# A preln graph layer on one core: three groups of ScalarE instructions change places in the edge step

## The reference

```python
h  = max(layernorm(x), 0)
em = relu(LN(concat(h[src], h[dst]) @ msg_w + msg_b) * msg_g + msg_beta) * edge_weight
messages = segment_mean(em, dst)                   # zero where no edge arrives
gate  = sigmoid(h @ gate_w + gate_b)
h_new = relu(LN(concat(h, messages) @ upd_w + upd_b) * upd_g + upd_beta)
out   = x + gate * h_new + (1 - gate) * h
```

## Time and profile before

| | us |
|---|---|
| three runs | 982.22, 986.97, 993.64 |
| their median | 986.97 |
| the profiled execution, own time | 981.87 |
| its span, first to last instruction | 980.1 |

### The profile page before, as it was taken

The page is one execution under the profiler, slowest core; times in us unless marked ns, Lnnn a source line. Parts: engine busy times, 40 slices in busy tenths (PEclk is TensorE's granted clock), DMA queues, the critical chain, the costliest instruction groups (busy, mean ns, idle before and its releaser), DMA issues.

```text
span 980.1 us, 19229 instructions
## 1 busy us (share of the span) xinstructions
PE 698.9 (71%) x3696; PEld 547.5 (56%) x3696; DVE 873.4 (89%) x3834; ACT 852.0 (87%) x3678; POOL 673.0 (69%) x602
## 2 busy tenths in 40 slices
PE   2377787877777777886766377777867878687781
PEld 1255555555555555554555266666756766576661
DVE  7299999999989999999995379999998888879984
ACT  3299999999989999999996389999989888779963
POOL 4667777776876877878747566766766666666557
PEclk9655655565555555556567698999899889889976
DMA  5246666666666667667523112333221111111111
GB/s 150 90 147 216 203 215 218 204 222 204 227 223 213 215 219 239 222 220 237 174 67 103 51 43 88 97 98 97 77 75 65 64 59 62 65 64 60 57 70 34
DMA packets 74260, 133.65 MB, mean 136 GB/s; under 512 B 15846, under 2 KB 17718, under 8 KB 74194
## 3 DMA queue, kind: packets, MB, share of 16 engines
q1 hardware_dynamic: 53868, 97.58, 28.6%
q0 software_dynamic: 18912, 34.84, 13.0%
q10 hardware_dynamic: 1414, 0.53, 0.2%
HBM read 56.01 MB, written 80.81 MB: 140 GB/s over the span
## 4 chain that ended last, share of the span: by engine, by line
ACT 45%; DVE 23%; issue 12%; PE 9%; another core or an unknown queue 6%; POOL 3%; ACTq 1%; DVEq 0%; DMA 0%; POOLq 0%; SPq 0%
ACT junk L410 13%; ACT hrow L403 9%; ACT work L437 8%; DVE work L458 5%; DVE work L469 5%; ACT xload L403 4%; POOL out L615 3%; DVE work L480 3%; ACT lnv L385 3%; DVE st L357 3%; ACT work L1134 2%; DVE work L475 2%; ACT rs L390 2%; PE pm L1273 2%
## 5 line engine op out<-in xcount | busy, mean ns | idle before, releaser
L615 POOL DMA_INDIRECT out<-work,sidx x196 | 201.4, 1027 | 128.0 <-issue 55.0
L1221 PE MATMUL pt<-ident,hrow 128*128 128x128 f32 x508 | 128.3, 401 | 128.9 <-ACT hrow L403 108.8
L610 POOL DMA_INDIRECT ring<-in_x,gidx x140 | 171.0, 1221 | 60.7 <-issue 41.1
L437 ACT ACTIVATE work<-work,gt 128x128 f32<-128x128 f32 x588 | 200.7, 413 | 3.7 <-DVE work L475 3.3
L1255 PE MATMUL py<-w_u,work 128*128 128x129 f32 x784 | 200.0, 434 | 0.0
L1255 PEld LDWEIGHTS py<-w_u,work 128*128 128x128 f32 x784 | 171.6, 322 | 39.2 <-issue 39.2
L610 POOL DMA_INDIRECT ring<-in_x,src_i x116 | 143.0, 1233 | 46.4 <-issue 34.4
L1221 PEld LDWEIGHTS pt<-ident,hrow 128*128 128x128 f32 x508 | 84.8, 202 | 159.3 <-ACT hrow L403 135.6
L410 ACT ACTIVATE junk<-py 128x128 bf16<-128x128 f32 x588 | 152.5, 278 | 18.5 <-remote 14.0
L469 DVE SCALAR_TENSOR_TENSOR work<-py,rs,g_upd 128x128 f32<-128x128 f32 x588 | 162.9, 336 | 4.2 <-ACT rs L390 4.2
L403 ACT ACTIVATE hrow<-xload,nb,rs 128x128 f32<-128x128 f32 x392 | 161.9, 489 | 3.0 <-DVE nb L396 2.7
(11 more groups left out here) (172 smaller groups left out, 1631.9 us busy)
## 6 DMA issues: line engine op xcount, KB each, us to landing
xload<-in_x SPq DMA_DIRECT2D x98, 256.0 KB
normalised_rows<-hrow SPq DMA_DIRECT2D x98, 256.0 KB
out<-work SPq DMA_DIRECT2D x98, 256.0 KB
running_sums<-acc SPq DMA_DIRECT2D x49, 256.0 KB
staged_target_rows<-work SPq DMA_DIRECT2D x14, 256.0 KB
ring<-staged_target_rows SPq DMA_DIRECT2D x14, 256.0 KB
out<-work,sidx POOLq DMA_INDIRECT x196
ring<-in_x,gidx POOLq DMA_INDIRECT x140
```

Source lines behind the costliest of these rows:

```text
L437: last = nc.scalar.activation(t_buf[:, g.at % 4, k, :], t_buf[:, g.at % 4, k, :], ACT.Relu, scale=gt[:, g.at % 4, k:k + 1])
L610: pool.indirect_dma_start(out=dest, out_offset=None, in_=rows, in_offset=bass.IndirectOffsetOnAxis(ap=idx, axis=0), **({} if rows is sums_ ...
L615: pool.indirect_dma_start(out=out, out_offset=bass.IndirectOffsetOnAxis(ap=idx, axis=0), in_=rows, in_offset=None, **if_tail).then_inc(s, 16)
L1221: last = nc.tensor.transpose(dest[:, k * H:(k + 1) * H], rows[:, k, :], ident[:, :])
```

## The change

It changes places in ScalarE's `edge_step` alone. `post` of s-6 moves from behind the third evacuation to ahead of the first one; the evacuation of `pa` moves from ahead of `post` to behind the first rows of L403. In the steps that have no node part the new order is: L385, L390, post (L410 on `py`, L418), L1132, L1134, L403 (first part), L1074, L427, L403 (second part), and the rest as before.

```diff
@@ edge_step of ScalarE
                     logs(act, nd, node, 2 * G)
                     rstds(act, nd, node, 2 * G)
+                if live(s.back(6), EG):
+                    post(act, ed, s.back(6), (s.at + 1) % 4, 3 * G, G, 1.0)
                 g = s.back(2)
                 if live(g, EG):
                     ed["flip"].after(act, g, 1)
...
                     if live(node.back(6), NG):
                         gated_relu(act, nd, node.back(6))
-                g = s.back(5)
-                if live(g, EG):
-                    evacuate(ed, g, at_[:, g.at % 2, :], pa[:, :], ACT.Copy, "at", "aflip")
-                if live(s.back(6), EG):
-                    post(act, ed, s.back(6), (s.at + 1) % 4, 3 * G, G, 1.0)
                 g = s.back(1)
...
                 if node is not None:
                     node_h(node)
+                q = s.back(5)
+                if live(q, EG):
+                    evacuate(ed, q, at_[:, q.at % 2, :], pa[:, :], ACT.Copy, "at", "aflip")
                 if live(s.back(6), EG):
                     gates(act, s.back(6), 0)
```

## The result

Slower. Four runs of the changed kernel have a median of 1004.65 us (997.89 to 1006.34), four of the kernel before in the same comparison 990.31 us (982.22 to 997.27); the ratio is 1.0158, with a 95% interval of 1.0080 to 1.0236. That is some 15 us, where the forecast was 7, and just inside the upper end of the range (1005.0). Every ratio in this document leaves out runs that are over 1.5% above the fastest of their kernel, so it can differ from that of the medians. The profiled execution of the changed kernel took 997.89 us, with a span of 996.2 and a granted clock of 0.688 over it (before: 980.1 and 0.706).

What follows compares the result with a forecast made beforehand. ScalarE and GpSimd's mean round were taken as level in the first stretch, GpSimd's round as the bound in the second; 5.1 + 2.0 + 0.3 = 7.4 us on 986.97 gave 994.4, rounded to 994.0, range 977 to 1005.

Steps and rivals of the forecast that it cites:

- the second stretch: Late edge-phase rounds set by GpSimd: four slow-clock rounds cost 3 x 1.2 + 1.54 = 5.1 us.
- the filled-wait rival: At L1134's idle time: upd is not held with flip 2, post runs inside the wait; 10 us faster, 977; chance 0.20.
- The move of the sums: Sums evacuated behind L403's first rows: cost 0 in the rounds, at most 1.6 us a step.
- the drain: Steps 51 to 53, where the sums' evacuation is directly on the path: 0.3 us slower, bounds 0 and 2.
- At full clock … 7.74, still inside 8.16: cost 0: Release to flip 2 grows from 6.20 by 1.54 to 7.74 us, within GpSimd's one-gather round of 8.16: no cost.
- with two gathers (9.47) nothing: At half clock the lengthened path of 9.3 us costs nothing against GpSimd's two-gather round of 9.47.
- The low-clock round with one gather: At half clock the path of 9.3 us passes GpSimd's 8.16: some 1.2 us a round.
- The first stretch: Edge-phase steps where ScalarE and GpSimd's mean round are level: ScalarE wants its first mark 0.48 earlier; 2.0 us slower.
- the bound of 3.8: Upper limit of the first stretch's cost: eight steps that stall today, 8 x 0.48 = 3.8 us.
- TensorE's marks reach the others only when GpSimd's run of indirect transfers is over: Edge phase: marks are released about 2.1 us behind the start of GpSimd's last gather, closing a round of 8.16 or 9.47.
- The rival of the held message mark: Before the squares on `pm`: the message product's mark is held too; 9 us more, 1003; chance 0.15.
- Lateness in one round is partly paid back by the next: Across rounds: the reason given for rounding the forecast from 994.4 to 994.0 us.

Runs made afterwards that it cites:

- e1: Only post moved ahead of the evacuations, the sums' evacuation left behind L1134, against the kernel before: 1030.47 us against 1014.5, ratio 1.0150.
- e11: post placed between the evacuations L1132 and L1134, sums evacuated right behind L1134, against the kernel before: 998.11 us against 993.2, ratio 1.0048.
- e2: Only the sums' evacuation moved behind the first rows of L403, post left in place, against the kernel before: 1013.67 us, ratio 0.9995.
- e5: The whole new order from step 50 on alone, otherwise the kernel before: 990.75 us against 993.2, ratio 0.9992.
- e7: Kernel before with GpSimd's 52 refill gathers replaced by plain loads on SyncE (wrong rows, same work for other engines): 964.2 us against 989.47, ratio 0.9746.
- e6: The whole new order in steps 30 to 49 alone, otherwise the kernel before: 997.41 us against 989.47, ratio 1.0105.
- e14: The whole new order in steps 8 to 29 alone, otherwise the kernel before: 999.82 us against 992.47, ratio 1.0069.
- e8: Changed kernel with the refill gathers replaced by plain loads on SyncE (wrong rows): 976.81 us, ratio 0.9868 to the kernel before.
- e13: Kernel before without GpSimd's wait for flip 2 of group g+6, so runs of two groups can join: 1065.96 us against 993.2, ratio 1.0720.
- e9: Changed kernel with TensorE turning the sums four times in place of once: 1002.24 us against the kernel before's 989.47, ratio 1.0148.

## Why the prediction was right or wrong

**What held.** The sign, the place and, in the second stretch, the mechanism. There most of TensorE's marks leave some 2 us behind the start of GpSimd's last gather, upd together with flip 2 (903.93 in the timeline above), so `post` did not fit into the wait and came onto the path: the filled-wait rival fell (e1, e11). The path itself was sized right: from release to flip 2 I had 7.74 at full clock and 9.3 at the lower one, and the profile of after has 903.28 - 895.50 = 7.78, and 832.67 - 823.31 = 9.36 in the round with a clock of 0.81. The move of the sums costs nothing that can be seen (e2), nor does the drain (e5), for which I had 0.3. The forecast of what the profile would show mostly came true: idle time before the first squares on `py`, one-gather rounds at the lower clock near 9 us, `hrow`'s waits gone; but full-clock ones are not all "still 8.1". The Trainium skill ("Perfetto Trace Analysis", Tensor Engine Instruction) says that a matmul's end in a profile is an estimate, so the matmuls themselves might be late. This trace speaks against it: in a round that isn't held ScalarE starts 0.04 behind the estimated end, three marks whose matmuls end 0.43 apart arrive 0.06 apart, and without the gathers ScalarE waits for flip 2 in 4 of steps 31 to 44 and not in all 14, in three of them 0.04 behind the matmul (e7).

**What failed: the size of two terms.** Both were 7.1 us together and measure 17 (10.4 and 6.8).

*The second stretch, "At full clock … 7.74, still inside 8.16: cost 0" and "with two gathers (9.47) nothing".* I had 5.1 from four rounds at the lower clock; e6 measures 10.4. The path was compared with GpSimd's round as if the two ran apart and the longer one counted. They share a mark, and who is released by it changes from round to round. A start that TensorE sets has GpSimd begin 1.18 behind ScalarE in place of 0.81, so the round is 8.43 to 8.50 and not 8.04 to 8.15 even at full clock, and the one with two gathers 9.87 and not 9.46 to 9.52. Each such start costs up to 0.4; there are five, 1.8 us in all. The low-clock round with one gather was priced at 1.2; the three of them cost 8.95 - 8.1 = 0.85 each. With two gathers it was priced at nothing: three times that is so (9.50 to 9.54, at a clock of 0.82), and once, at 0.67, it took 10.35, 0.85 over the 9.5 of before. The prediction had the slow rounds mostly with one gather; in this profile four of the eight have two. The eighth, behind the last gather, was not in the sum and is the dearest: 8.94 in place of 7.13, 1.8 us. Together that is some 7 us; less the 1.1 that before itself loses in its round at 0.63 (9.17 from 854.78 on) it is the 6 by which the fourteen rounds differ. The windows of six rounds above show each kind. Steps 45 to 49, which I left out, lose 2.5 (36.8 to 39.3), in two places: step 45 takes 8.86 in place of 7.44, which is mostly this last round, and step 49 takes 8.16 in place of 7.09. Steps 46 to 48 take 7.44 in both: the loop of 7.34 leaves 0.1 a step in which a lateness could be regained.

*The first stretch, "Here ScalarE comes to L1134 mostly later than the mark … I take 2.0".* e14 measures 6.8, over the bound of 3.8, which its interval only just reaches. The bound counted the eight steps that stalled before and multiplied them by 0.48, the earlier want of a mark. But 1.54 is also added to the loop of ScalarE and TensorE, and at the lower clock that loop (7.34 at full clock, 8.92 in the round at 0.81) passes ScalarE's own step, which is 8.64 by the stages and was 8.75 in the prediction. The path of 9.3 at the lower clock stood in the prediction too, and was set against GpSimd alone. e8 shows this without gathers: steps of 8.9 to 9.0, and of 10.3 to 10.6 behind a longer low stretch, where e7 has 8.64.

*"TensorE's marks reach the others only when GpSimd's run of indirect transfers is over"* is too general. The first rows of the timeline above have a mark in the midst of a run: the last product for `py` ends at 603.38, and ScalarE starts at 603.46, 0.61 behind the start of a gather that takes 1.02. In e13 too the mark of 849.25 is passed on at 849.29, between the scatters of 848.88 and 850.17. By the semaphores' records of after, 24 of 32 marks of the message product whose matmul ends between two transfers of a run are there within 0.1 us. In the second stretch upd and flip 2, which end under the run's last transfers, are mostly held; what decides it no run here shows.

*The rival of the held message mark* was seen once in the profile of after: at step 26 ScalarE waits 2.94 us for `pm`, whose product had ended at 744.66, until 748.11, 2.34 behind the start of the gather of 745.77; and five times, 3.1 us in all, for the product itself. The profile of e14 has it once too, 1.53 us. It looks like a small part, but no run takes it out, and that it explains some us of the 15 can't be excluded.

*"Lateness in one round is partly paid back by the next"* held less than thought: to regain a lateness a full-clock round had 8.16 - 6.20 = 1.96 us before, and has 8.16 - 7.78 = 0.38 after.

**What stays open.** How the rise of the time at the lower clock (68 to 85 us) and the loss feed each other; the doses (5 us for 1.06, 15 for 1.54) look like it, and e9 speaks against the clock as the whole reason, but e9 is not clean. And the split between the switches and the low-clock rounds is read from one profile of each kernel, not measured by a run. Why some marks are held under a run and others pass is open as well.

## What to carry to other kernels

When an engine's wait looks like room for other work, ask what ends the wait: if the mark for the work comes in the same moment as the mark that is waited for, the work goes onto the path and not into the gap. Then set the longer path against every loop that shares a mark with it, at the lower clock as well and in rounds of each kind, not against the one that is the bound today. Two loops within some tenths of a us of each other lost here at each change of lead, so slack should not be spent to its last tenths.

## What the runs showed of the hardware

In the second stretch TensorE's semaphore marks for ScalarE and GpSimd were mostly held while GpSimd issued indirect transfers one behind the other: they came 1.6 to 2.2 us behind the start of the run's last gather, several within 0.1 us of each other (13 of 14 in before, 9 of 14 in after). Other marks passed within such a run without delay (603.46 in after, 849.29 in e13). Where two groups' runs joined, a mark came 8.0 us after its matmul (e13), and that kernel was 7.2% slower though a wait had been taken out of it. Replacing 52 gathers with loads on SyncE made the kernel 2.5% faster (e7), although GpSimd was not the fullest engine: with it the held marks of the second stretch went, from 13 in 14 steps to one (e7). And four turns of the sums in place of one raised TensorE's granted clock from 0.86 to 0.93 in the second stretch without any gain in time (e9).
